# Reordering a feed-forward turn: route, choice and mixing ahead of the masked passes, the input sums at its start

## The chip, the core and the metric

One core of a Trainium2 chip runs the whole kernel. The metric is the device time of one execution in microseconds, lower is better. Engines are named as in the profile: PE (TensorE matmul), PEld (its weight loads), DVE (VectorE), ACT (ScalarE), POOL (GpSimd), SP (SyncE, which here only issues transfers).

## What is computed

An input x of shape (2, 4096, 256) goes through a feed-forward with half a residual, an attention, and the same feed-forward again:

```python
x = x + 0.5 * ffn(layernorm(x))
x = x + attention(layernorm(x))
x = x + 0.5 * ffn(layernorm(x))

def ffn(x):
    x_mixed = k[0] * x_before + k[1] * x + k[2] * x_behind        # along the sequence
    h = einsum('bsd,pdm->bspm', x_mixed, W1) + b1                  # 9 paths of width 64
    stacked = einsum('bspm,pmd->bspd', h, W2) + b2
    scores = tanh(x_mixed @ Wo1 + bo1) @ Wo2 + bo2
    collapsed = stacked of the path argmax(scores)
    return layernorm(x + collapsed) * gamma + beta
```

The change is in the feed-forward alone.

## The kernel before

Both feed-forwards (`ph` 0 and 1) run the same code over 16 tiles of 512 rows. Each engine's program is a list of turns, `for t in turns()`, from -6 to 16, fully unrolled, and inside a turn the order of the work is written out by hand, one `turn(t)` for each engine (DVE L814, ACT L1132, PE L1414, POOL L556, SP's loop behind L425). Engines meet only through semaphores. A turn works on several tiles at once, at the distances `STATS, ROWS, MIX, ROUTE, HIDDEN = 6, 5, 3, 2, 1`:

- tile t+6: DVE takes the input sums (`input_sums`, four BATCH_NORM_STATS2, recorded at L693) and moments (L700) of the rows in x; POOL makes scale and shift of them (`norm_scale`, L521 to L533).
- tile t+5: ACT writes the normalised rows n (L1071), PE transposes them (L1332), ACT copies the transposes to nT (L1077).
- tile t+3: ACT scales the middle tap of the mixing (L1085), DVE adds the tap before (`mixed_before`, L732) and behind (`mixed_behind`, L740), ACT rounds to f16 (`x_high`, L1093), DVE takes the remainder (`mixed_low`, L747).
- tile t+2: PE multiplies the hidden block 0 (`hidden(t, 0)`), which holds the scores' hidden layer and path 0; ACT does tanh (L1101) and keeps path 0 in hb (L1105); PE makes the nine scores (`route`, L1389); DVE finds the best in five small route steps (`route(t, 0)` to `route(t, 4)`, L777, L780, L784, L787, L790), which end in a one-hot; PE transposes it (`choice`, L1398), ACT copies it (`one_hot`, L1113), SP stores it to DRAM and loads it back three times as the mask of the tile (`spread`, L407 to L416).
- tile t+1: PE multiplies hidden blocks 1 to 4; DVE masks blocks 0 to 4 (`masked`, L802 and L805), ACT rounds them to f16 in three groups, blocks 0 and 1, 2 and 3, and 4 (`masked_high`, L1121), DVE takes the remainders (`masked_low` 0, 1 and 2, L811).
- tile t: PE multiplies by W2 (`path` 0 to 4). All split products on PE are at L1324.
- tile t-1: DVE adds the result to n (`result`, L753), ACT squares it (L1129), POOL makes 1/std (`result_scale`, L540 and L544), DVE scales it (`result_scaled`, four of L762) and adds x plus beta (`result_added`, L770), SP stores it (L423).

POOL's `residual` (L553) adds beta to the rows in x, 128x1024 f32, before `result_added` reads them. It waits for masked 3 of its tile.

x has eight tile buffers (`x_rows(t)` is t % NT, NT = 8). So SP loads tile t+7 in turn t, at the end of it, behind `store(t - 1)`, which waits for `result_added(t - 1)`, the last reader of that buffer. The input sums of tile t+7 come in turn t+1, in DVE's order behind masked 3. Tiles 0 to 7 of a feed-forward are loaded ahead of the turns (in the second, tiles 0 to 4 already within the attention).

PE has three banks for hidden blocks; `h_order` lists the blocks in PE's order, and each waits until the one three places earlier has been read. `hidden(t + ROUTE, 0)` opens PE's turn, `path(t, 4)` closes it. `path(t, 0)` waits for `result(t - 1)`, since both use the same two banks.

DVE's turn before, in order: result; masked 0, 1; mixed before (two); route 0; masked low 0; route 1; masked 2; route 2; mixed behind; route 3; mixed behind; route 4; masked 3; the four input sums; mixed low; masked 4; moments; masked low 1; result scaled (four); masked low 2; result added.

## Time and profile before

| what | us |
|---|---|
| median of three runs | 1528.1 (1524.33 to 1539.24) |
| profiled execution, its time | 1531.81 |
| profiled execution, span from first to last instruction | 1530.0 |
| first result pass to the last one, first feed-forward | 69.2 to 328.0 |
| the same, second feed-forward | 1271.1 to 1519.3 |

Shares of the span: PE 89%, DVE 79%, ACT 61%, POOL 20%; mean granted clock of PE 0.967. In the profile, starts are counted from the first instruction; an instruction's time overlaps the start of the next on its engine by some 0.1 us, so the time from start to start is what an instruction costs its engine. "idle before" is time in which an engine had nothing to run, and the name behind it is what ended that wait. PEclk is PE's granted clock, 1.00 being 2.4 GHz and 0.50 being 1.2 GHz.

### The profile page before, as it was taken

The numbers are of one execution on the slowest core, as the hardware profiler recorded it, in microseconds if no ns is written. First come the engines' busy times: TensorE is split into PE (matmuls) and PEld (weight loads), VectorE is DVE, ScalarE is ACT, GpSimd is POOL, SyncE is SP. The second block draws the span as 40 slices with busy tenths as digits, with TensorE's granted clock in tenths as the row PEclk, the third lists the DMA queues.
The fourth block names the chain that finished last, engine by engine and source line by source line (L and its number), as shares of the span: only waits on it lengthen the run. The fifth ranks groups of instructions, "written<-read, shape, count | busy, mean of one in ns | idle before, by whom it ended". The sixth has DMA issues, their size and how long they took to land.

```text
span 1530.0 us, 25980 instructions
## 1 busy us (share of the span) xinstructions
PE 1359.1 (89%) x7700; PEld 781.4 (51%) x7700; DVE 1215.7 (79%) x2349; ACT 936.8 (61%) x1745; POOL 306.9 (20%) x359
## 2 busy tenths in 40 slices
PE   4889988858999999999968999999998779989985
PEld 2556666544554454545344455454444346656653
DVE  6989999766677677677866767777678769999985
ACT  5656665326567666566855666766666666666642
POOL 2244452332001000000041101000000214444311
PEclk9989999979999999999989999999999879999997
DMA  5143333320000100102110011000103112333221
GB/s 155 43 118 88 90 101 113 90 69 1 28 29 15 41 14 15 32 11 74 37 43 1 28 42 42 0 28 0 42 0 110 56 32 61 103 97 106 61 74 57
DMA packets 86994, 82.26 MB, mean 54 GB/s; under 512 B 8540, under 2 KB 86885, under 8 KB 86885
## 3 DMA queue, kind: packets, MB, share of 16 engines
q1 hardware_dynamic: 86884, 80.91, 17.8%
q8 instruction: 56, 0.92, 0.3%
q14 instruction: 54, 0.43, 0.1%
HBM read 55.43 MB, written 25.46 MB: 53 GB/s over the span
## 4 chain that ended last, share of the span: by engine, by line
PE 62%; DVE 11%; DMA 10%; issue 7%; ACT 6%; SPq 2%; POOL 1%; DVEq 0%; ACTq 0%; POOLq 0%
PE PS L1324 55%; DMA R<-oh_scratch 7%; PE PS L1501 3%; DMA oh_scratch<-oh_t 2%; DVE R L753 2%; PE PS L1389 2%; PE PS L1332 1%; DVE R L770 1%; DVE R L937 1%; SPq L414 1%; SPq L412 1%; ACT oh_t L1113 1%; ACT R L1211 1%; ACT R L1215 1%; ACT R L1174 1%
## 5 line engine op out<-in xcount | busy, mean ns | idle before, releaser
L1324 PE MATMUL PS<-R 128*128 128x512 f16 (+3 forms) x3456 | 713.6, 361 | 27.4 <-DVE R L937 17.3
L1324 PEld LDWEIGHTS PS<-R 128*128 128x128 f16 (+1 forms) x3456 | 326.0, 98 | 392.3 <-DVE R L937 32.0
L1324 PE MATMUL PS<-w_hi,R 128*128 128x256 f16 x1280 | 239.1, 280 | 63.3 <-DVE R L753 63.1
L937 DVE TENSOR_TENSOR R<-R 128x512 f16<-128x512 f32 (+3 forms) x288 | 188.6, 655 | 111.5 <-ACT R L1215 110.3
L1202 ACT ACTIVATE R<-PS 128x512 f32 (+5 forms) x288 | 160.2, 558 | 162.7 <-PE PS L1324 162.2
L1324 PE MATMUL PS<-R,w_hi 128*128 128x512 f16 x640 | 198.0, 392 | 1.6 <-DVE R L747 1.5
L1211 ACT ACTIVATE R<-R 128x512 f32 (+4 forms) x288 | 169.5, 589 | 48.3 <-DVE R L931 46.8
L931 DVE TENSOR_TENSOR R<-R,max_row 128x512 f32 (+4 forms) x288 | 187.1, 650 | 7.7 <-ACT max_row L1248 7.7
L1215 ACT ACTIVATE R<-R 128x512 f16<-128x512 f32 (+3 forms) x288 | 171.1, 594 | 28.6 <-ACT R L1211 2.6
L925 DVE TENSOR_TENSOR run_max<-run_max,R 128x512 f32<-128x512 f32 (+3 forms) x272 | 173.9, 639 | 10.0 <-DVE run_max L925 1.7
L1324 PEld LDWEIGHTS PS<-w_hi,R 128*128 128x128 f16 x1280 | 128.4, 100 | 104.5 <-DVE R L753 77.1
L1324 PE MATMUL PS<-w_lo,R 128*128 128x256 f16 x640 | 179.0, 280 | 0.0
L1121 ACT ACTIVATE R<-R 128x1024 f16<-128x1024 f32 (+1 forms) x96 | 87.3, 909 | 146.4 <-DVE R L805 146.4
L521 POOL TENSOR_SCALAR veps<-mv 128x4 f32<-128x4 f32 x48 | 29.3, 610 | 690.5 <-DVE mv L700 631.0
L1324 PE MATMUL PS<-R,w_lo 128*128 128x512 f16 x320 | 124.7, 390 | 0.0
L805 DVE SCALAR_TENSOR_TENSOR R<-PS,b1c,R 128x512 f32<-128x512 f32 x128 | 95.0, 742 | 18.9 <-PE PS L1324 17.2
L811 DVE TENSOR_TENSOR R<-R 128x1024 f16<-128x1024 f32 (+1 forms) x96 | 98.4, 1028 | 2.4 <-ACT R L1121 2.4
L1332 PE MATMUL PS<-ident,R 128*128 128x128 f32 x384 | 64.3, 319 | 37.3 <-ACT R L1071 28.9
L553 POOL TENSOR_TENSOR R<-R,beta_b 128x1024 f32<-128x1024 f32 x32 | 75.7, 2365 | 105.5 <-DVE R L805 105.5
L1324 PEld LDWEIGHTS PS<-R,w_hi 128*128 128x128 f16 x640 | 63.8, 104 | 54.8 <-issue 7.1
L747 DVE TENSOR_TENSOR R<-R 128x1024 f16<-128x1024 f32 x32 | 73.9, 2310 | 2.9 <-ACT R L1093 2.9
L1332 PEld LDWEIGHTS PS<-ident,R 128*128 128x128 f32 x384 | 52.1, 164 | 47.0 <-issue 21.6
(109 smaller groups left out, 1555.3 us busy)
## 6 DMA issues: line engine op xcount, KB each, us to landing
R<-x_scratch SPq DMA_DIRECT2D x48, 512.0 KB, 4.5
x_scratch<-R SPq DMA_DIRECT2D x32, 512.0 KB, 3.2
R<-oh_scratch SPq DMA_DIRECT2D x32, 320.0 KB
R<-in_L_attn_x SPq DMA_DIRECT2D x16, 512.0 KB, 5.4
R<-oh_scratch SPq DMA_DIRECT2D x32, 256.0 KB
out<-R SPq DMA_DIRECT2D x16, 512.0 KB, 3.2
R<-in_L_ffn_W SPq DMA_DIRECT2D x2, 288.0 KB
R<-in_L_ffn_W SPq DMA_DIRECT2D x1, 512.0 KB
```

The lines of the kernel that those rows point to most:

```text
L553: g.tensor_tensor(rows4(x_rows(t)), rows4(x_rows(t)), beta_b[:, :].unsqueeze(1).to_broadcast([P, SUB, D]), ALU.add).then_inc(xb_done, 1)
L805: v.scalar_tensor_tensor(out=at, in0=ps_h[:, h_bank[g, c], :], scalar=b1c[:, c:c + 1], in1=chunk(mask, t, c), op0=ALU.add, op1=ALU.mult).t ...
L811: v.tensor_tensor(chunk(hlo, t, c, n), cols(hm, c * TT, n * TT), chunk(hhi, t, c, n), ALU.subtract)\
L925: v.tensor_tensor(run_max[:, lo:], run_max[:, lo:], cols(ring, at, TT - lo), ALU.max)\
L931: v.tensor_tensor(cols(ring, at, TT - lo), cols(ring, at, TT - lo), max_row[:, lo:], ALU.subtract)\
L937: v.tensor_tensor(p_lo[:, i * TT + lo:(i + 1) * TT], pf[:, (i % 2) * TT + lo:(i % 2 + 1) * TT], p_hi[:, i * TT + lo:(i + 1) * TT], ALU.sub ...
L1121: a.activation(chunk(hhi, t, c, n), cols(hm, c * TT, n * TT), ACT.Copy).then_inc(hhi_done, 1)
L1202: a.activation(cols(ring, ring_m + i * TT + lo, TT - lo), ps_s[:, i, lo:], ACT.Abs, scale=1.0 / (QS * XS * D ** 0.5)).then_inc(abs_done, 1)
L1211: a.activation(p, cols(ring, ring_n + i * TT + lo, TT - lo), ACT.Exp)\
L1215: a.activation(p_hi[:, i * TT + lo:(i + 1) * TT], p, ACT.Copy).then_inc(phi_done, 1)
L1324: ins = t_.matmul(dst, w, xx, start=start and n == 0, stop=stop and n == last, skip_group_check=skip)
L1332: ins = t_.transpose(dst[:, u * P:(u + 1) * P], cols(rows, u * D + c * P, P), ident[:, :])
```

## The change

DVE's turn after: result; route 0, input sum 0, route 1, input sum 1, route 2, input sum 2, route 3, input sum 3, route 4; mixed before (two); moments; mixed behind (two); masked 0, 1; mixed low; masked low 0; masked 2, 3, 4; masked low 1; result scaled; masked low 2; result added. PE opens with the scores (`route`) and puts the transposes of the one-hot (`choice`) behind path 0; hidden block 0 moves from the start of turn t+1 to the end of turn t, ahead of path 4. ACT takes tanh, the middle tap, squares, the one-hot, the normalised rows, x_high, then the three masked groups and nT. POOL's residual of tile t now waits for path 4 of tile t-1 (`o_psum`), and stands first in POOL's turn t. The mask loads count on two semaphores, one for even and one for odd tiles. Lines left out are marked by "...":

```diff
--- before.py
+++ after.py
@@ -35,6 +35,8 @@
...
 STATS, ROWS, MIX, ROUTE, HIDDEN = 6, 5, 3, 2, 1
+
+FIRST = ROUTE + 1
 
...
@@ -196,7 +198,7 @@
...
         route_psum, route_step, oh_done = sem("route_psum"), sem("route_step"), sem("oh_done")
-        ohT_psum, ohT_done, oh_stored, mask_in = sem("ohT_psum"), sem("ohT_done"), sem("oh_stored"), sem("mask_in")
+        ohT_psum, ohT_done, oh_stored, mask_in = sem("ohT_psum"), sem("ohT_done"), sem("oh_stored"), [sem("mask_in0"), sem("mask_in1")]
         hm_done, hhi_done, hlo_done = sem("hm_done"), sem("hhi_done"), sem("hlo_done")
...
@@ -345,8 +347,8 @@
...
             for t in turns():
-                h_order += [(use(ph, t + ROUTE), 0)] if on(t + ROUTE) else []
                 h_order += [(use(ph, t + HIDDEN), c) for c in range(1, HC)] if on(t + HIDDEN) else []
+                h_order += [(use(ph, t + FIRST), 0)] if on(t + FIRST) else []
         h_bank = {x: i % H_BANKS for i, x in enumerate(h_order)}
...
@@ -403,17 +405,17 @@
...
                     if g >= 2:
-                        sp.wait_ge(mask_in, 16 * MASK_LOADS * (g - 1))
+                        sp.wait_ge(mask_in[g % 2], 16 * MASK_LOADS * (g // 2))
                     sp.dma_start(there, oh_t[:, :]).then_inc(oh_stored, 16)
...
                     sp.dma_start(m[DM:P, :, :], there[0::2, :].unsqueeze(0).to_broadcast([DM, HC, TT]))\
-                        .then_inc(mask_in, 16)
+                        .then_inc(mask_in[g % 2], 16)
                     sp.dma_start(m[0:DM, 1:, :], there[1::2, :].unsqueeze(0).to_broadcast([DM, HC - 1, TT]))\
-                        .then_inc(mask_in, 16)
-                    sp.dma_start(m[0:NP, 0, :], there).then_inc(mask_in, 16)
+                        .then_inc(mask_in[g % 2], 16)
+                    sp.dma_start(m[0:NP, 0, :], there).then_inc(mask_in[g % 2], 16)
 
...
@@ -549,15 +551,14 @@
...
                     pool.wait_ge(n_done, k + 1)
-                    pool.wait_ge(hm_done, HC * k + 4)
+                    if t >= 1:
+                        pool.wait_ge(o_psum, k)
                     g.tensor_tensor(rows4(x_rows(t)), rows4(x_rows(t)),
...
                 def turn(t):
-                    if on(t - 1):
-                        result_scale(t - 1)
-                    if on(t + HIDDEN):
-                        residual(t + HIDDEN)
+                    if on(t):
+                        residual(t)
                     if on(t + STATS) and not early(ph, t + STATS):
...
@@ -566,6 +567,8 @@
...
                         first_scales(0, first_of(ph, t))
+                    if on(t - 1):
+                        result_scale(t - 1)
 
...
@@ -716,12 +719,15 @@
...
 
-                def input_sums(t):
+                def input_sum(t, u):
                     n = counted(ph, t)
-                    dve.wait_ge(x_in[t % NT], 16 * loads(ph, t))
-                    if n >= 2:
-                        dve.wait_ge(n_shift, n - 1)
-                    row_sums(X, t % NT * SUB * D, rows_set(ph, t), n_stat)
+                    if u == 0:
+                        dve.wait_ge(x_in[t % NT], 16 * loads(ph, t))
+                        if n >= 2:
+                            dve.wait_ge(n_shift, n - 1)
+                    ins = v.bn_stats(st[:, rows_set(ph, t), u, :], cols(x_rows(t), u * D, D))
+                    if u == SUB - 1:
+                        ins.then_inc(n_stat, 1)
 
...
@@ -797,7 +803,7 @@
...
                     if c == 0:
-                        dve.wait_ge(mask_in, 16 * MASK_LOADS * (g + 1))
+                        dve.wait_ge(mask_in[g % 2], 16 * MASK_LOADS * (g // 2 + 1))
                         dve.wait_ge(hb_done, g + 1)
...
@@ -818,43 +824,31 @@
...
                         result(t - 1)
+                    for i in range(SUB + 1):
+                        if choice:
+                            route(t + ROUTE, i)
+                        if rows and i < SUB:
+                            input_sum(t + STATS, i)
+                    if mix:
+                        mixed_before(t + MIX, 0)
+                        mixed_before(t + MIX, 1)
+                    if rows:
+                        input_moments(t + STATS)
+                    elif first_of(ph, t):
+                        first_stats(0, first_of(ph, t))
+                    if mix:
+                        mixed_behind(t + MIX, 0)
+                        mixed_behind(t + MIX, 1)
                     if here:
...
                     if mix:
-                        mixed_before(t + MIX, 0)
-                        mixed_before(t + MIX, 1)
-                    if choice:
-                        route(t + ROUTE, 0)
+                        mixed_low(t + MIX)
                     if here:
                         masked_low(t + HIDDEN, 0)
-                    if choice:
-                        route(t + ROUTE, 1)
-                    if here:
                         masked(t + HIDDEN, 2)
-                    if choice:
-                        route(t + ROUTE, 2)
-                    if mix:
-                        mixed_behind(t + MIX, 0)
-                    if choice:
-                        route(t + ROUTE, 3)
-                    if mix:
-                        mixed_behind(t + MIX, 1)
-                    if choice:
-                        route(t + ROUTE, 4)
-                    if here:
                         masked(t + HIDDEN, 3)
-                    if rows:
-                        input_sums(t + STATS)
-                    elif first_of(ph, t):
-                        first_stats(0, first_of(ph, t))
-                    if mix:
-                        mixed_low(t + MIX)
-                    if here:
                         masked(t + HIDDEN, 4)
-                    if rows:
-                        input_moments(t + STATS)
-                    if here:
                         masked_low(t + HIDDEN, 1)
...
@@ -1135,26 +1129,24 @@
...
                         act.wait_ge(w1_ready, 1)
+                    if choice:
+                        scores(t + ROUTE)
                     if mix:
                         middle(t + MIX)
-                    if choice:
-                        scores(t + ROUTE)
-                    if here:
-                        masked_high(t + HIDDEN, 0)
                     if last:
                         squares(t - 1)
+                    if choice:
+                        one_hot(t + ROUTE)
                     if on(t + ROWS):
...
                         x_high(t + MIX)
-                    if choice:
-                        one_hot(t + ROUTE)
                     if here:
+                        masked_high(t + HIDDEN, 0)
                         masked_high(t + HIDDEN, 1)
+                        masked_high(t + HIDDEN, 2)
                     if on(t + ROWS):
                         transposed(t + ROWS)
-                    if here:
-                        masked_high(t + HIDDEN, 2)
 
...
@@ -1412,19 +1404,17 @@
...
                 def turn(t):
-                    here, second, first = on(t), on(t + HIDDEN), on(t + ROUTE)
-                    if ph == 0 and t == -ROUTE:
-                        pe.wait_ge(w1_ready, 1)
+                    here, second, choose = on(t), on(t + HIDDEN), on(t + ROUTE)
                     if ph == 0 and t == 0:
                         pe.wait_ge(w2_ready, 1)
-                    if first:
-                        hidden(t + ROUTE, 0)
+                    if choose:
+                        route(t + ROUTE)
                     if second:
...
                         path(t, 0)
-                    if first:
-                        route(t + ROUTE)
+                    if choose:
+                        choice(t + ROUTE)
                     if second:
...
@@ -1433,14 +1423,17 @@
...
                         path(t, 2)
-                    if first:
-                        choice(t + ROUTE)
-                    if on(t + ROWS):
-                        transposed(t + ROWS)
                     if second:
...
                         path(t, 3)
+                    if on(t + ROWS):
+                        transposed(t + ROWS)
+                    if ph == 0 and t == -FIRST:
+                        pe.wait_ge(w1_ready, 1)
+                    if on(t + FIRST):
+                        hidden(t + FIRST, 0)
+                    if here:
                         path(t, 4)
```

## Rows read from the trace of the kernel before

**Rows 1.** Timeline of DVE in turn 6 of the first feed-forward (start us, us, engine, line, what).
```profile
161.08 1.21 DVE L753 SCALAR_TENSOR_TENSOR R<-PS,R 128x1024 f32<-128x1024 f32 x1
...
164.80 0.18 DVE L777 TENSOR_REDUCE r_max<-PS 128x4 f32<-128x36 f32 x1
164.91 1.21 DVE L811 TENSOR_TENSOR R<-R 128x1024 f16<-128x1024 f32 x1
...
168.58 0.75 DVE L805 SCALAR_TENSOR_TENSOR R<-PS,b1c,R 128x512 f32<-128x512 f32 x1
169.25 1.39 DVE L693 BATCH_NORM_STATS2 st<-R 128x6 f32<-128x256 f32 x4
170.56 2.37 DVE L747 TENSOR_TENSOR R<-R 128x1024 f16<-128x1024 f32 x1
...
174.91 1.66 DVE L762 SCALAR_TENSOR_TENSOR R<-R,y_rstd,gamma_b 128x256 f32<-128x256 f32 x4
...
178.24 1.21 DVE L753 SCALAR_TENSOR_TENSOR R<-PS,R 128x1024 f32<-128x1024 f32 x1
```

**Rows 2.** Timeline of PE in the same turn: path 0, route, hidden block 2, next path 0.
```profile
162.35 0.28 PE L1324 MATMUL PS<-w_hi,R 128*128 128x256 f16 x1 [1.80 <-DVE R L753]
...
163.67 0.96 PE L1389 MATMUL PS<-wo,th 65*128 65x9 f32 x8
164.48 0.59 PE L1324 MATMUL PS<-R,w_hi 128*128 128x512 f16 x2
...
179.50 0.28 PE L1324 MATMUL PS<-w_hi,R 128*128 128x256 f16 x1 [1.80 <-DVE R L753]
```

**Rows 3.** Instructions of L747 over the whole kernel (duration in ns min/median/max).
```profile
L747 DVE TENSOR_TENSOR R<-R x32: 1203/2370/3415, 23.9 to 1468.5; 128x1024 f16<-128x1024 f32 x32
```

**Rows 4.** Timeline of POOL in turn 6.
```profile
169.48 2.37 POOL L553 TENSOR_TENSOR R<-R,beta_b 128x1024 f32<-128x1024 f32 x1 [1.78 <-DVE R L805]
...
176.25 2.15 POOL L530 TENSOR_SCALAR neg<-mv 128x4 f32<-128x4 f32 x1
```

**Rows 5.** Timeline of ACT in turn 6.
```profile
170.70 1.04 ACT L1121 ACTIVATE R<-R 128x1024 f16<-128x1024 f32 x1
```

**Rows 6.** Timeline of SP at the start of turn 6.
```profile
161.19 0.41 SPq L423 DMA_DIRECT2D x_scratch<-R  x1
161.64 0.51 SPq L398 DMA_DIRECT2D R<-in_L_attn_x  x1
```

**Rows 7.** Transfer issues, 150 to 200 us and 1290 to 1440 us; then L398 alone, whole kernel.
```profile
R<-in_L_attn_x SPq DMA_DIRECT2D x3, 512.0 KB, 4.6
...
R<-x_scratch SPq DMA_DIRECT2D x8, 512.0 KB, 4.6
...
DMA to landing us min/median/max: 4.0/5.0/9.1
```

**Rows 8.** PE after two idle times, and windows beside them (busy us of PE, PEld, DVE, ACT, POOL; PEclk; DMA).
```profile
89.18 0.39 PE L1324 MATMUL PS<-w_hi,R 128*128 128x256 f16 x1 [2.86 <-DVE R L753]
...
1510.07 0.40 PE L1324 MATMUL PS<-w_hi,R 128*128 128x256 f16 x1 [3.88 <-DVE R L753]
...
93.00:98.00 5.00, 5.00 (x19) 2.72 (x20) 3.33 (x8) 2.10 (x6) 1.23 (x2) 0.50 0.13 44
98.00:103.00 5.00, 5.00 (x36) 3.37 (x35) 3.52 (x8) 2.47 (x3) 2.14 (x1) 0.94 0.00 1
1510.00:1520.00 10.00, 9.17 (x60) 7.05 (x60) 3.63 (x7) 1.70 (x8) 1.21 (x2) 0.74 0.31 102
```

**Rows 9.** Timeline of DVE: result passes that open turns 2 and 10 of each feed-forward.
```profile
87.91 1.21 DVE L753 SCALAR_TENSOR_TENSOR R<-PS,R 128x1024 f32<-128x1024 f32 x1
...
229.70 1.21 DVE L753 SCALAR_TENSOR_TENSOR R<-PS,R 128x1024 f32<-128x1024 f32 x1
...
1288.99 1.21 DVE L753 SCALAR_TENSOR_TENSOR R<-PS,R 128x1024 f32<-128x1024 f32 x1
...
1426.29 1.21 DVE L753 SCALAR_TENSOR_TENSOR R<-PS,R 128x1024 f32<-128x1024 f32 x1
```

## The prediction

> **What bounds the kernel now.** I read the page first for the engines' shares, then the Vector engine's timeline for one feed-forward turn, then SyncE's, GpSimd's and TensorE's timelines for the same turn. Vector is without a gap: the turn whose result pass starts at 161.08 ends when the next one starts at 178.24, 17.16 us, and nearly all of turns 2 to 9 of each feed-forward, which matter below, repeat it (this is turn 6 of the first) [rows 1]. TensorE idles 1.80 us in it, waiting for the result pass (L753), and works 15.35 us [rows 2]. So Vector sets the pace, and one of its instructions is slower than its kind: L747 takes 2.37 us as a rule and 1.20 at best [rows 3]. GpSimd's residual pass (L553, 169.48 to 171.85) lies across its start at 170.56 [rows 1, 4]; L747 ends 1.08 us after that pass does. Vector thus loses 1.17 us a turn to GpSimd. The input sums (L693) just ahead of it, beside the same pass, take 1.39 us for four and lose nothing.
>
> **The change part by part.** All offsets are from the start of the result pass.
>
> GpSimd's pass. It now waits for the end of the previous tile's paths (o_psum) instead of masked 3, and comes beside the result pass (1.14 us to the next start) and the input sums. L747 goes back to 1.20: minus 1.17. What could come late instead is route step 2, with two small operands in SBUF, at offset 2.0: at most the rest of the pass, 0.4 us, and nothing where the input sums wait longer than the pass lasts (below). The Trainium skill (GPSIMD Engine Reference, Key points) says that GpSimd contends with Vector instructions that have two SBUF inputs; the rows agree for L747. By that rule alone, the result pass, with one input in PSUM, would be free of it, as I take it; no row shows that pair, and its price is bounded by 0 and by the pass itself, 2.37.
>
> Masked passes in one run. Masked low 1 now stands right behind masked 4. It needs ScalarE's copy of the group of masked 3, 1.04 us [rows 5], and only masked 4 (0.67 us from start to start [rows 1]) lies between: about 0.5 us of new wait, counting 0.1 for two handovers. Masked low 0 has mixed low in front (1.1 us) against the same copy: 0.1. The bounds are 0, if the copies finish early, and 1.2, if nothing covers them.
>
> Input sums first. This is the part that decides. SyncE issues the store of x1 and then the load of tile t+7 only when the last pass of turn t (L770) is over, since that pass reads the buffer which the load overwrites: 161.19 and 161.64, that is 0.1 and 0.55 us behind the start of the next turn's result pass [rows 6]. The load lands 4.6 us after its issue, in the first feed-forward and in the second [rows 7], so at offset 5.15. Today the first input sum of that very tile stands at 169.25, offset 8.2, and the load has 3 us to spare. After the change it stands behind the result pass and route step 0, at 1.14 + 0.11 = 1.25 (a route step takes 0.11 from start to start, 164.80 to 164.91 [rows 1]). Vector waits from 1.25 to about 5.2: 3.95 us. Nothing hides it: Vector executes in order, and route steps 1 to 4, the mixing and all masked passes are queued behind that sum. The wait falls on tiles 8 to 15, the ones reloaded into the eight x buffers, so on turns 2 to 9 of either feed-forward: 16 turns. Turns 0 and 1, and those past 9, need no such load. The store issued just before the load shares the transfer engines with it; the bounds are the quickest and the slowest landing of that line, 4.0 and 9.1 us [rows 7]; I take the 4.6 of these very stages.
>
> The Trainium skill (DMA: Bandwidth & Descriptors, Rules for kernel authors) says to issue a transfer early and to wait for it late; this edit does the opposite for the x load. The same page (Anatomy of one DMA, Where 436 GB/s comes from) gives 2 us of fixed cost and some 358 GB/s from HBM; my estimate from that is 3.5 us for 512 KB, which would make the wait 2.85 and the total 18 us less. The trace's 4.6 us is used.
>
> Vector's turn by itself: 17.16 - 1.17 + 0.6 + 3.95 = 20.5 us, and about 0.1 more for handovers. I take 20.6.
>
> Route and choice first. The choice's transposes on TensorE now follow path 0. Path 0 starts at 1.27 and takes 1.32, route 0.81, a hidden block 1.3 [rows 2]. So TensorE is through path 0 at 2.6 and then has to wait for the one-hot (route step 4). The four sums (1.39 us) and steps 1 to 4 (0.45) follow the load, so that is done at about 7.1. TensorE stands still from 2.6 to 7.2, 4.6 us in one piece. It has 15.35 - 1.3 - 0.8 - 1.3 = 11.95 us of work left of the turn and is done at 19.2, 1.4 us before Vector. At the full clock this wait costs nothing.
>
> But the clock falls in such gaps. TensorE idled 2.86 us before 89.18, and the granted clock was 0.50 from 93 to 98 and 0.94 from 98 to 103, so at the lower of the two levels (1.2 GHz) until about 98.6, 9.4 us after it went on [rows 8]. Before 1510.07 it idled 3.88 us, and the clock was 0.74 in the stretch 1510 to 1520, which is 5.2 us at the lower level [rows 8]. Half the speed for 5.2 to 9.4 us costs TensorE 2.6 to 4.7 us; the 1.4 of slack takes a part, which leaves 1.2 to 3.3 a turn; 0 if the clock holds. I take 1.4, near the shorter one, because the gaps will come in every turn and recoveries can't all be long. The turn becomes 22.0 us.
>
> The per-parity mask semaphores add no instruction. The masks' way (store of the one-hot, three loads) starts some 1.5 us earlier in the turn and is used later: cost 0. The loads are no longer in flight just ahead of the x load. Beginning hidden 0 at the end of the turn instead of the start of the next is the same work; turn 2 of today's first feed-forward holds that loss of clock at 89.18, and its time is in the sum below as it was.
>
> Turns past 9. TensorE no longer transposes new tiles, so o_psum comes 1 to 2 us sooner and can meet Vector's four scaled-result instructions (L762), two SBUF inputs each. GpSimd's pass then takes its 2.2 us out of Vector in some turns: 0 to 4 turns in each feed-forward, 0 to 18 us, and against it L747's loss goes in those turns too. I take plus 8. The fill gains the waits for masks and loses at the mix: 0, give or take 3.
>
> **Sum.** Turns 2 to 9 last 229.70 - 87.91 = 141.8 us in the first feed-forward and 1426.29 - 1288.99 = 137.3 in the second [rows 9], 279.1 together. 16 x 22.0 = 352.0: plus 73. With the end's 8 and 3 less for turns 0 and 1: plus 78. The profiled execution took 1531.8 us (span 1530.0), the median of the runs is 1528.1: 1610 for a profiled one, 1606 as a median.
>
> **The rivals.**
> 1. The wait for the load alone, the clock holds. For: TensorE's slack of 1.4 us hides a short loss, and the gap of 1.80 before 179.50 [rows 2] goes by in every turn. Against: the gaps will be 4.6 us, and those of 2.86 and 3.88 each cost the clock. 16 x 20.6 = 330: plus 51, 1579 or, with the end's share gone, 1574.
> 2. GpSimd's pass gets hold of SBUF before the result pass. o_psum comes about 1.4 us before Vector's turn ends, while it is in L770 or one pass ahead of it. For: nothing in the code ties the pass to the result pass. Against: a small GpSimd instruction that began at 176.25, beside L762, ended only at 178.40 (2.15 us), when the next result pass had begun at 178.24 [rows 1, 4]: the two-input passes between had kept it out, and the same two (masked low 2, L770) stand there after the change. Should the pass go first, Vector loses 2.2 us in nearly every turn, part of which covers the clock's loss: 16 x 23 + 10 x 2, about plus 110: 1635.
> 3. The other side: the load is there in time and the kernel gets faster. The turn would then be 20.6 - 3.95 = 16.65, and 16 turns 266 instead of 279, minus 13, with the end about minus 8: 1520. It decides from a wait under 0.5 us, that is with the load landed at offset 1.8. Against: it is issued at 0.55 and the quickest took 4.0 us. For: only that the wait of one line is not yet in any trace.
>
> **How the numbers follow.** The forecast (load plus clock) 0.58, rival 1 0.22, rival 2 0.13, rival 3 0.04, and 0.03 for no change by some mixture. A measurement tells about 1% from no change here. Slower by over 1%: 0.93; within 1%: 0.04; faster: 0.03. The range: down to 1565 (clock holds, the load at 4.0 us), up to 1645 (rival 2, or 9 us of low clock each turn).
>
> **What would show it.** Right: the first L693 of turns 2 to 9 waits some 4 us for the x load (DMA R<-in_L_attn_x or x_scratch), turns of 21 to 23 us; TensorE's L1398 waits over 4 us for L790; L747 at 1.2 us; the granted clock under 0.9 in these turns. Wrong: no idle time ahead of L693, or turns below 18 us. A residual pass that begins while L762 runs, with L762 or L770 over 2 us long, would be rival 2; a clock of 1.00 beside 20.6 us turns rival 1.

## The result, and the profile after

| | median us (range) | profiled execution: time, span | PE clock |
|---|---|---|---|
| before | 1526.21 (1524.13 to 1539.24) | 1531.81, 1530.0 | 0.967 |
| after | 1606.98 (1603.35 to 1610.81) | 1607.41, 1605.6 | 0.947 |

The ratio is 1.0511, with a 95% interval of 1.0446 to 1.0575: 5% slower. The forecast said 1606.

I read the profile after in the order of the prediction: Vector's timeline, SyncE's, TensorE's, the clock by stretches, and then the ends, which the forecast had treated lightly. Lines have moved: L753, L693, L747, L762 and L398 of before are L759, L728, L753, L768 and L400 now.

Vector in turn 6 of the first feed-forward, which answers to [rows 1] (timeline of DVE; start us, us, engine, line, what, idle time before and its releaser):

```profile
176.78 1.22 DVE L759 SCALAR_TENSOR_TENSOR R<-PS,R 128x1024 f32<-128x1024 f32 x1
...
181.91 0.43 DVE L728 BATCH_NORM_STATS2 st<-R 128x6 f32<-128x256 f32 x1 [3.82 <-DMA R<-in_L_attn_x]
...
187.93 1.23 DVE L753 TENSOR_TENSOR R<-R 128x1024 f16<-128x1024 f32 x1
...
192.33 0.75 DVE L811 SCALAR_TENSOR_TENSOR R<-PS,b1c,R 128x512 f32<-128x512 f32 x1 [0.70 <-PE PS L1316]
```

The next result pass starts at 197.45, so this turn took 20.67 us instead of 17.16. The first input sum stands idle for 3.82 us; mixed low takes 1.23 us instead of 2.37. SyncE's timeline says why the sum waits:

```profile
176.89 0.41 SPq L425 DMA_DIRECT2D x_scratch<-R  x1
177.34 0.51 SPq L400 DMA_DIRECT2D R<-in_L_attn_x  x1
```

The group of the sums over the whole kernel (busy us, mean ns, then all idle time before them by releaser) says how much that is in all:

```profile
L728 DVE BATCH_NORM_STATS2 st<-R 128x6 f32<-128x256 f32 x108 | 44.2, 418 | 73.0 <-DMA R<-in_L_attn_x 34.7 <-DMA R<-x_scratch 33.4 <-issue 4.6
```

The load is issued 0.56 us behind the start of the result pass and the sum runs at 5.13, against 0.55 and 5.15 in the prediction. 34.7 + 33.4 = 68.1 us are 17 waits; 1.9 us of it belongs to the kernel's very first load, and the 16 waits of turns 2 to 9 are 66.2 us, 4.1 us each (3.6 to 5.5).

TensorE, which answers to [rows 2] (timeline of PE):

```profile
183.77 0.59 PE L1390 MATMUL PS<-ident,oh 128*9 128x128 f16 x4 [4.02 <-DVE oh L796]
```

The granted clock around it and over turns 2 to 9 (windows: stretch, its us, busy us and count of PE, PEld, DVE, ACT, POOL, then PEclk, DMA share, GB/s):

```profile
179.00:183.70 4.70, 0.75 (x7) 0.42 (x5) 1.79 (x9) 0.74 (x4) 0.10 (x1) 0.97 0.50 141
183.70:187.00 3.30, 3.23 (x12) 1.35 (x13) 3.30 (x10) 2.60 (x6) 1.40 (x2) 0.52 0.01 3
187.00:190.00 3.00, 3.00 (x24) 2.12 (x22) 2.97 (x4) 1.96 (x2) 2.82 (x3) 1.00 0.63 171
...
111.33:134.70 23.37, 17.89 (x113) 11.64 (x112) 16.14 (x33) 11.67 (x23) 8.39 (x8) 0.85 0.24 72
176.78:197.45 20.67, 16.65 (x113) 11.01 (x112) 16.12 (x33) 11.67 (x23) 8.40 (x8) 0.92 0.29 81
...
89.90:261.30 171.40, 135.99 (x876) 89.61 (x873) 129.00 (x257) 92.41 (x175) 67.19 (x57) 0.89 0.27 78
1328.54:1500.97 172.43, 136.35 (x876) 89.92 (x873) 128.96 (x257) 92.44 (x175) 67.17 (x57) 0.89 0.26 78
```

TensorE stands 4.02 us, then works at 0.52, the lower level (1.2 GHz), for some 3.3 us; masked 4 pays with 0.70 us of waiting. Over turns 2 to 9 the clock is 0.89 in both feed-forwards.

The turn read is one of the milder ones. The last two pairs of lines show turn 3, turn 6, and turns 2 to 9 of either feed-forward. Ten of the 16 turns have a clock of 0.92, which is 3.3 us at the lower level, and take 20.9 us on average; the other six have 0.84 or 0.85, which is some 7 us at the lower level, and take 22.5. Turn 3, with 0.85, takes 23.37 us: its load lands 6.0 us behind its issue, so that the first sum waits 5.27 us, and masked 4 waits 1.92 us for TensorE.

**Where the 75.6 us of span came from**, by the starts of the result passes (before against after): turns 2 to 9, 141.8 to 171.4 and 137.3 to 172.4, together +64.7, a mean turn of 21.5; from turn 10 to the last result pass +5.1 and +1.0; turn 1, 18.7 to 16.9 and 17.8 to 16.9, -2.8; and the stretches ahead of the first result pass of each feed-forward, +3.8 and +3.8 (69.22 to 73.02, and from the last result pass of the first feed-forward to the first of the second, 943.1 to 946.9). That is 64.7 + 6.1 - 2.8 + 7.6 = 75.6.

### The profile page after: what moved, and what is told of

It reads as the page before. It is cut to its first block, busy times and chain, and to the rows that moved or that the text cites. A ratio compares the mean times of both kernels' runs of the same rounds, so it can differ in the third digit from the quotient of the medians.

```text
span 1605.6 us, 25980 instructions
## 1 busy us (share of the span) xinstructions
PE 1385.4 (86%) x7700; PEld 789.3 (49%) x7700; DVE 1202.7 (75%) x2349; ACT 944.0 (59%) x1745; POOL 334.0 (21%) x359
## 4 chain that ended last, share of the span: by engine, by line
PE 60%; DVE 20%; issue 6%; ACT 6%; DMA 5%; SPq 1%; POOL 1%; ACTq 0%; DVEq 0%; POOLq 0%
PE PS L1316 54%; PE PS L1494 3%; DVE R L768 3%; DMA R<-x_scratch 2%; DMA R<-in_L_attn_x 2%; DVE R L817 2%; DVE R L776 2%; DVE R L811 2%; DVE st L728 2%; DVE R L931 1%; PE PS L1324 1%; ACT R L1203 1%; ACT R L1115 1%; ACT R L1207 1%; ACT R L1166 1%
## 5 line engine op out<-in xcount | busy, mean ns | idle before, releaser
L1316 PE MATMUL PS<-w_hi,R 128*128 128x256 f16 x1280 | 253.2, 287 | 36.4 <-DVE R L759 36.4
L1316 PE MATMUL PS<-R,w_hi 128*128 128x512 f16 x640 | 210.3, 413 | 5.6 <-DVE R L753 2.9
L523 POOL TENSOR_SCALAR veps<-mv 128x4 f32<-128x4 f32 x48 | 17.8, 370 | 828.3 <-DVE mv L703 671.2
L1316 PE MATMUL PS<-w_lo,R 128*128 128x256 f16 x640 | 183.6, 287 | 0.0
L1316 PEld LDWEIGHTS PS<-w_hi,R 128*128 128x128 f16 x1280 | 132.3, 103 | 79.6 <-DVE R L759 41.9
L1316 PE MATMUL PS<-R,w_lo 128*128 128x512 f16 x320 | 131.9, 412 | 0.0
L556 POOL TENSOR_TENSOR R<-R,beta_b 128x1024 f32<-128x1024 f32 x32 | 91.5, 2860 | 187.5 <-PE PS L1316 187.5
L728 DVE BATCH_NORM_STATS2 st<-R 128x6 f32<-128x256 f32 x108 | 44.2, 418 | 73.0 <-DMA R<-in_L_attn_x 34.7
L1123 ACT ACTIVATE R<-R 128x256 bf16<-128x256 f32 x128 | 51.6, 404 | 71.0 <-DVE R L759 71.0
```

Of the source, the lines that this page charges most:

```text
L556: g.tensor_tensor(rows4(x_rows(t)), rows4(x_rows(t)), beta_b[:, :].unsqueeze(1).to_broadcast([P, SUB, D]), ALU.add).then_inc(xb_done, 1)
L1316: ins = t_.matmul(dst, w, xx, start=start and n == 0, stop=stop and n == last, skip_group_check=skip)
```

## The experiments

Each run is given with its ratio to the kernel before, taken on the same chip, and with "T", the mean length of turns 2 to 9 of both feed-forwards by the starts of the result passes. For comparison: before T = 17.4 (with one turn of 21.7 us at a clock of 0.76; 17.16 otherwise), after T = 21.5.

**1. The sums behind the mixing.** The kernel after, with the four sums and the moments moved:

```diff
-                        if rows and i < SUB:
-                            input_sum(t + STATS, i)
                     if mix:
                         mixed_before(t + MIX, 0)
                         mixed_before(t + MIX, 1)
+                        mixed_behind(t + MIX, 0)
+                        mixed_behind(t + MIX, 1)
                     if rows:
+                        for u in range(SUB):
+                            input_sum(t + STATS, u)
                         input_moments(t + STATS)
...
-                    if mix:
-                        mixed_behind(t + MIX, 0)
-                        mixed_behind(t + MIX, 1)
```

> The changed kernel with one part undone: the four input sums and the moments stand behind the mixing again (offset about 5.5 us of a turn), the five route steps back to back in front. If the wait for the x load is the cause, it ends before the sums come: the idle time ahead of the input sums (3.85 us in the changed kernel) falls below 0.3 us, PE's gap ahead of the one-hot transposes to under 1.5 us, the clock stays up, turns 2 to 9 take 17.2 to 17.6 us (not less than before, since route step 2 now stands in GpSimd's pass), and the kernel comes to 1530 to 1550 us. If another part of the change carries the loss (the masked passes in one run, the later choice), turns stay over 20 us and the kernel over 1590 us.

Measured: 1574.65 us, ratio 1.0296 (1.0264 to 1.0327), T = 19.0. The load's wait is nearly gone (none in seven of the 16 turns, 0.2 to 1.0 us in eight, 1.7 in one) and the time falls by 32 us, but this is far above the 1530 to 1550 expected. Turns of about 17.6 and 19.96 us mostly alternate. Vector's and GpSimd's timelines in a long turn and at the start of a short one:

```profile
164.18 3.77 DVE L768 SCALAR_TENSOR_TENSOR R<-R,y_rstd,gamma_b 128x256 f32<-128x256 f32 x4
...
183.88 1.67 DVE L768 SCALAR_TENSOR_TENSOR R<-R,y_rstd,gamma_b 128x256 f32<-128x256 f32 x4
...
164.66 2.62 POOL L556 TENSOR_TENSOR R<-R,beta_b 128x1024 f32<-128x1024 f32 x1 [2.61 <-PE PS L1315]
...
185.55 3.95 POOL L556 TENSOR_TENSOR R<-R,beta_b 128x1024 f32<-128x1024 f32 x1 [3.80 <-PE PS L1315]
```

Where GpSimd's pass falls among the four scaled-result passes, these take 3.77 us instead of 1.67. That is the prediction's rival 2, which the load's wait had hidden in turns 2 to 9: with Vector 3.9 us late, o_psum never came so early in Vector's turn. Where the pass is ready one step later (185.55), behind the scaled results, it records 3.95 us and keeps waiting while masked low 2 and the result's addition run one behind the other.

**2. The load ahead of the store.** The kernel after, with SyncE's two issues swapped:

```diff
-                        store(t - 1)
...
+                            sp.wait_ge(x1_done, use(ph, t - 1) + 1)
                             load_rows(t - 1 + NT)
+                        store(t - 1)
```

> The changed kernel with the x load issued ahead of the store on SyncE, both still behind the last reader of the buffer. Load theory: issued 0.45 us sooner and with the store behind it instead of in front, it lands 3.2 to 3.7 us after the start of the result pass instead of 5.1, the wait of the input sums falls to 2.0 to 2.5 us, each of the 16 turns by 1.4 to 1.9 us or a little more with the clock, and the kernel to 1570 to 1585 us. If the wait were set by something else (the shared input path, n_shift), nothing changes: 1603 to 1611 us.

Measured: 1593.58 us, ratio 1.0419 (1.0387 to 1.0451), T = 20.5. SyncE's issue, the waits of the sum and of masked 4 (DVE), and the one-hot's (PE), in the timelines of one turn:

```profile
173.62 0.40 SPq L400 DMA_DIRECT2D R<-in_L_attn_x  x1
...
178.00 0.43 DVE L731 BATCH_NORM_STATS2 st<-R 128x6 f32<-128x256 f32 x1 [3.17 <-DMA R<-in_L_attn_x]
...
189.65 0.75 DVE L814 SCALAR_TENSOR_TENSOR R<-PS,b1c,R 128x512 f32<-128x512 f32 x1 [1.93 <-PE PS L1319]
...
179.86 0.59 PE L1393 MATMUL PS<-ident,oh 128*9 128x128 f16 x4 [3.59 <-DVE oh L799]
```

The load's landing in turns 2 to 9 of the first feed-forward, in the kernel after and then in this run:

```profile
DMA to landing us min/median/max: 4.5/4.6/6.0
...
DMA to landing us min/median/max: 4.2/4.4/4.5
```

The load is issued 0.45 us sooner and lands 0.2 us faster (the medians of the second feed-forward are 4.5 and 4.3). It is there 4.49 us behind the start of the result pass, not at the 3.2 to 3.7 expected, and that is why the 13 us won are less than the 22 to 37 expected. The wait shrinks by 0.65 us in the turn read and by 0.9 on average (4.1 to 3.2), and T falls by 1.0. The turns swing between 19.6 and 21.4: those at a clock of 1.00 take 19.6 to 19.9 us, those at 0.84 take 21.2 to 21.4, with masked 4 waiting 1.93 us for TensorE in the one read.

**3. TensorE kept busy in the gap.** The kernel after, with hidden block 2 multiplied three more times ahead of the choice in turns 2 to 9 (same bank, same values, about 3.9 us of extra work at the full clock):

```diff
                         path(t, 0)
+                    if 2 <= t <= 9:
+                        for i in range(3):
+                            hidden(t + HIDDEN, 2, spare=True)
                     if choose:
```

> The changed kernel, where PE repeats hidden block 2 three times more (3.9 us, into the bank that the real one then overwrites) in turns 2 to 9, between path 0 and the choice, where it waits. Adds work to PE and takes none away. Clock theory: the gap shrinks from 4.0 us to about 0.4, the granted clock stays at 1.00 in turns 2 to 9, the turns fall from 21.5 us on average to 20.5, the kernel by 12 to 20 us to 1587 to 1595 us. If the clock's fall costs nothing (PE's slack covers it), the time stays within 4 us of the changed kernel, 1603 to 1611 us, or rises.

Measured: 1593.21 us, ratio 1.042 (1.0389 to 1.0451), T = 20.5, as the clock theory wanted. The window of a turn, and of turns 2 to 9:

```profile
173.96:194.41 20.45, 19.25 (x130) 12.28 (x128) 16.09 (x33) 11.47 (x22) 9.59 (x8) 1.00 0.28 82
...
91.62:255.90 164.28, 154.10 (x1026) 98.26 (x1024) 128.82 (x257) 91.81 (x176) 76.76 (x57) 1.00 0.29 82
1323.84:1487.16 163.32, 154.10 (x1026) 98.25 (x1024) 128.82 (x257) 91.81 (x176) 76.77 (x57) 1.00 0.28 82
```

TensorE has more to do and the kernel is 14 us faster. Every turn now takes 20.3 to 20.8 us: Vector's own turn with the load's wait in it, which the prediction had put at 20.6. The fallen clock costs 21.5 - 20.5 = 1.0 us a turn. About 0.3 of that is the load's wait, 3.9 us on average here and 4.1 in the kernel after: the late landings of the long turns are gone too. Why a load lands late there was not tried.

**4. GpSimd's pass tied to the result pass.** The kernel after, with one wait more on the residual pass, for the last pass of Vector's previous turn:

```diff
                         pool.wait_ge(o_psum, k)
+                        pool.wait_ge(x1_done, k - 1)
```

> The changed kernel, where GpSimd's residual pass also waits for x1_done of tile t-2, the last DVE pass of the turn before, so that it can't start beside the scaled result. Theory that the pass is let in between those instructions and holds them (four turns over 3.7 us for L768 in the changed kernel, 2.1 us each): all L768 groups take 1.67 us, and the turns past 9 get faster by 8 to 12 us in sum; turns 2 to 9 unchanged within 0.1 us each. Kernel 1595 to 1601 us. If those groups are long for another reason: unchanged, 1603 to 1611 us.

Measured: 1596.14 us, ratio 1.0447 (1.0414 to 1.048), T = 21.3 (21.32 against 21.49): as expected. All 32 passes of GpSimd now take 2.34 to 2.37 us (2.34 to 4.41 in the kernel after), and at the ends the scaled results take 1.67 us again instead of 3.77. From turn 10 to the last result pass the two feed-forwards are 5.0 and 5.2 us shorter than in the kernel after.

**5. Both: the sums behind the mixing and the pass with the result.**

> The kernel after with both of the earlier edits: the input sums and moments behind the mixing, and GpSimd's residual pass made to wait for the last pass of Vector's previous turn as well. The theory says that the first edit alone took away the wait for the load and let GpSimd's pass in among the four scaled-result passes in every second turn, which costs those turns 2.1 to 2.4 us (turns of 17.6 and 19.96 us in turn). With the second edit the pass starts beside the result pass in every turn, so all of turns 2 to 9 should take 17.2 to 18.0 us: 1.2 us less over 16 turns, 19 us, and some 10 us at the ends, as the second edit gave alone: 1540 to 1550 us from 1574.65. The rival (the long turns come from something else, as a late hidden block or the clock) has them stay at 17.6 and 20.0 in turn: 1565 to 1575.

Measured: 1548.67 us, ratio 1.014 (1.0103 to 1.0176), T = 18.3, with 13 of the 16 turns at 18.15 to 18.17. The alternation is gone, and so the 2.1 us in every second turn were GpSimd's. But 18.16 us a turn is above the 17.2 to 18.0 expected. The start of a turn in the timelines of DVE and POOL:

```profile
166.39 1.21 DVE L760 SCALAR_TENSOR_TENSOR R<-PS,R 128x1024 f32<-128x1024 f32 x1
167.52 0.18 DVE L784 TENSOR_REDUCE r_max<-PS 128x4 f32<-128x36 f32 x1
167.74 0.20 DVE L787 TENSOR_TENSOR r_eq<-PS,r_max 128x36 f32<-128x36 f32 x1
167.97 1.09 DVE L791 TENSOR_TENSOR r_pr<-r_eq,prio 128x36 f32<-128x36 f32 x1
169.09 0.19 DVE L794 TENSOR_REDUCE r_top<-r_pr 128x4 f32<-128x36 f32 x1
169.31 0.20 DVE L797 TENSOR_TENSOR oh<-r_pr,r_top 128x36 f16<-128x36 f32 x1
...
166.64 2.36 POOL L557 TENSOR_TENSOR R<-R,beta_b 128x1024 f32<-128x1024 f32 x1 [5.71 <-DVE R L777]
```

Route step 2 (L791), with its two operands in SBUF, is held for 0.89 us by the rest of GpSimd's pass; result pass and steps 0 and 1, which have one operand in PSUM, run through it. And a step that needs the one just before it starts 0.22 us behind it (not counting the held time), where a step followed by other work takes 0.11 [rows 1]: the four handovers cost some 0.4. With masked low 1's wait for its copy, 0.46, and about 0.25 of small gaps, 17.16 - 1.17 + 0.89 + 0.4 + 0.46 + 0.25 = 18.0; the turn is 18.16. So the route in one block costs 1.3 us a turn in itself. In the kernel after neither the held step nor the handovers show, since the sums lie between the steps and the load's wait outlasts the pass.

**6. Before, with nothing but the sums moved** right behind the result pass:

```diff
                         result(t - 1)
+                    if rows:
+                        input_sums(t + STATS)
```

> The kernel before with one edit: the four input sums stand right behind the result pass. Theory: the wait for the x load is a loss by itself, whatever the order of the rest: the first sum at offset 1.15, the load there at about 5.2, so 4 us a turn in turns 2 to 9, the masked passes and the mixing late by that. Turns of 21 to 22.5 us, L747 at 1.2 or 2.4 by where GpSimd's pass falls: 1528.6 plus 16 times 3.8 to 5.3: 1590 to 1613 us. The rival, that the wait costs only together with the choice in front (TensorE's gap), has Vector catch up: 1528 to 1560 us.

Measured: 1626.6 us, ratio 1.0648 (1.061 to 1.0687), T = 23.2: slower than the whole change, and above the expected range. DVE, then PE and POOL:

```profile
167.05 1.41 DVE L693 BATCH_NORM_STATS2 st<-R 128x6 f32<-128x256 f32 x4 [3.98 <-DMA R<-in_L_attn_x]
...
175.81 3.24 DVE L747 TENSOR_TENSOR R<-R 128x1024 f16<-128x1024 f32 x1 [0.36 <-ACT R L1093]
180.00 0.75 DVE L805 SCALAR_TENSOR_TENSOR R<-PS,b1c,R 128x512 f32<-128x512 f32 x1 [0.96 <-PE PS L1324]
...
174.85 0.59 PE L1398 MATMUL PS<-ident,oh 128*9 128x128 f16 x4 [4.21 <-DVE oh L790]
...
175.60 2.36 POOL L553 TENSOR_TENSOR R<-R,beta_b 128x1024 f32<-128x1024 f32 x1 [1.44 <-DVE R L805]
```

One edit brings the whole loss: 3.98 for the load; mixed low 0.87 longer and 0.36 idle, since with the sums no longer ahead of it GpSimd's pass lies across all of it; and TensorE's gap of 4.21 with masked 4's wait of 0.96 behind it. 17.16 + 3.98 + 0.87 + 0.36 + 0.96 = 23.3. The rival, that the wait needs the choice in front to hurt, falls.

**7. Before, with nothing but GpSimd's pass moved** (it waits for o_psum and comes first in its turn):

```diff
-                    pool.wait_ge(hm_done, HC * k + 4)
+                    if t >= 1:
+                        pool.wait_ge(o_psum, k)
```

> The kernel before with one edit: GpSimd's residual pass waits for the end of the previous tile's paths instead of masked pass 3, and comes first in its turn. It lies beside the result pass then, and behind that stands masked 0, with two operands in SBUF. Theory: what L747 gets back (1.17 us a turn) masked 0 loses, by the rest of the pass, 1.0 to 1.3 us, so the time stays: 1520 to 1536 us. If the result pass covered GpSimd's altogether, the gain of 1.17 us in some 28 turns would stand whole: 1495 to 1500. If the pass gets in among the scaled-result passes, as it does in the kernel after without the load's wait, turns take 1 us more: 1545 to 1560.

Measured: 1551.93 us, ratio 1.0168 (1.0131 to 1.0204), T = 17.4. DVE and POOL in a turn of the middle, and POOL and DVE at the end:

```profile
175.89 1.21 DVE L754 SCALAR_TENSOR_TENSOR R<-PS,R 128x1024 f32<-128x1024 f32 x1
177.03 2.26 DVE L803 TENSOR_TENSOR R<-R 128x512 f32<-128x512 f32 x1
...
186.80 1.20 DVE L748 TENSOR_TENSOR R<-R 128x1024 f16<-128x1024 f32 x1
...
176.39 2.35 POOL L554 TENSOR_TENSOR R<-R,beta_b 128x1024 f32<-128x1024 f32 x1
...
1483.93 3.76 DVE L763 SCALAR_TENSOR_TENSOR R<-R,y_rstd,gamma_b 128x256 f32<-128x256 f32 x4
...
1484.79 2.62 POOL L554 TENSOR_TENSOR R<-R,beta_b 128x1024 f32<-128x1024 f32 x1 [9.37 <-PE PS L1325]
```

The middle goes by the theory: mixed low is at 1.20, and masked 0 behind the result pass takes 2.26 instead of 0.67. The whole is that of the third alternative, because past turn 9 the pass gets in among the scaled results, in one turn of the first feed-forward and five of the second (18.0 to 21.2 us a turn in the second feed-forward, against 15.7 to 16.9 before).

**8. A candidate: masked 1 beside GpSimd's pass.** The kernel after with the pass tied to the result pass; Vector's order is result, route 0, masked 1, route 1 to 4, mixing, sums, masked 0, mixed low, and the rest with the moments behind masked 3; `result_scale` ahead of `norm_scale`.

> A candidate. The order behind the result pass: route step 0, masked 1 (one operand in PSUM), route steps 1 to 4, mixing, input sums, masked 0, mixed low, masked low 0, masked 2 and 3, moments, masked 4, masked low 1; the residual pass beside the result pass by the added wait, result_scale ahead of norm_scale on GpSimd. The load has until offset 7 or so, masked 1 stands beside the rest of GpSimd's pass, L747's like takes 1.2 us, the copy for masked low 1 has the moments and masked 4 ahead of it. Theory: Vector's turn is 17.16 less 1.17 plus up to 0.8 of waits, 16.2 to 16.9 us: 1505 to 1530 us. If the theory on where the time goes lacks a part, it stays above 1535.

Measured: 1526.91 us, ratio 0.9999 (0.9978 to 1.002), T = 17.1. The time is in the expected range, the turn above the 16.2 to 16.9 expected. Step 2 is now held for 0.37 us only, and the load is in time but for 0.6 us in two turns. The change's whole loss is gone, but not more. A steady turn is 17.0 us: 17.16 - 1.17 + 0.37 for the held step, some 0.4 for the handovers and 0.20 for masked low 1's wait. What turns 2 to 9 win by it, the stretches ahead of the first result passes lose (73.8 us against 69.2 in the first feed-forward, 947.1 against 943.1 in the second).

**9. The pass behind route step 4.** The kernel before, its order untouched, with one wait changed:

```diff
-                    pool.wait_ge(hm_done, HC * k + 4)
+                    if on(t + ROUTE - HIDDEN):
+                        pool.wait_ge(oh_done, use(ph, t + ROUTE - HIDDEN) + 1)
+                    else:
+                        pool.wait_ge(hm_done, HC * k + 4)
```

> A version that should beat both. The kernel before, its order untouched, with one wait changed: GpSimd's residual pass waits for route step 4 (the one-hot of the tile ahead) instead of masked 3. It then starts 0.85 us earlier and lies beside masked 3 and the input sums, none of which it held up in any trace, so that mixed low, which lost 1.17 us a turn, loses only some 0.3. Theory: turns 16.3 us instead of 17.16 in turns 2 to 9, and 0.9 us less in the others, 28 turns in all: 1500 to 1512 us. If the pass gets in before masked 3's neighbours with two SBUF operands (the mixing ahead of step 4), or mixed low waits for its own inputs, the time stays: 1520 to 1530.

Measured: 1518.65 us, ratio 0.9952 (0.9935 to 0.9969), T = 16.9: a gain, but not the 15 to 28 us expected. DVE and POOL:

```profile
164.11 1.39 DVE L696 BATCH_NORM_STATS2 st<-R 128x6 f32<-128x256 f32 x4
165.42 1.55 DVE L750 TENSOR_TENSOR R<-R 128x1024 f16<-128x1024 f32 x1
167.46 0.75 DVE L808 SCALAR_TENSOR_TENSOR R<-PS,b1c,R 128x512 f32<-128x512 f32 x1 [0.49 <-PE PS L1327]
...
163.52 2.37 POOL L556 TENSOR_TENSOR R<-R,beta_b 128x1024 f32<-128x1024 f32 x1 [0.96 <-DVE oh L793]
```

Mixed low is at 1.55, as worked out. What the expectation left out is the wait that this uncovers: masked 4 arrives sooner than TensorE's hidden block 4, 0.49 us of idle time. And past turn 9 no input sums stand ahead of mixed low, so there the pass still lies across it (2.58 us in turn 10), where the expectation had counted 0.9 us a turn.

**10. The same, and the moments ahead of mixed low.**

> The run before this one and also the moments (0.29 us, no operand pair in SBUF) ahead of mixed low, so that nothing of GpSimd's pass is left when mixed low starts. Theory: 0.3 us less in turns with input sums, some 17 turns: 1496 to 1508 us, 4 to 6 us under the run with the wait alone. The rival: the moments stand right behind the sums they read and wait for them, or masked low 1 waits for its copy by what the moments no longer cover, and nothing is won: within 2 us of that run.

Measured: 1517.37 us, ratio 0.9933 (0.9908 to 0.9958), T = 16.9 (16.65 in the second feed-forward alone). Mixed low is at 1.19 us, masked 4 waits 0.32. By the medians within 2 us of the run before it, though its steady turns are 0.26 us shorter: turns 1 and 2 of the first feed-forward took 18.7 and 20.0 us in its profile (17.9 and 16.9 in run 9) and gave that back. On the whole time alone the two can't be told apart.

**11. The choice behind path 1.** Run 4, with the transposes of the one-hot moved on TensorE:

```diff
-                    if choose:
-                        choice(t + ROUTE)
                     if second:
                         hidden(t + HIDDEN, 2)
                     if here:
                         path(t, 1)
+                    if choose:
+                        choice(t + ROUTE)
```

> The kernel after with the added wait of the residual pass (as in the run in which the pass was tied to the result pass, 1596.14 us) and the choice's transposes moved on TensorE from behind path 0 to behind path 1. Theory: the clock falls for TensorE's 4 us in one piece; with hidden block 2 and path 1 ahead of the choice TensorE idles less in one piece, the clock stays high, and the turn is Vector's own with the load's wait, 20.5 us in turns 2 to 9: 1580 to 1588 us. The rival, that turns of 21 to 23 come from elsewhere than the clock after that gap, has 1593 to 1600.

Measured: 1604.16 us, ratio 1.0496 (1.0455 to 1.0536), T = 20.6: the whole is outside both expectations. The turns are what the theory said: T was 21.3 in run 4, TensorE stands 1.64 us for the one-hot in the turn read, instead of 3.8 to 5.4 (timeline of PE), and the clock is 0.99 (window of turns 2 to 9 of the second feed-forward):

```profile
170.54 0.39 PE L1391 MATMUL PS<-ident,oh 128*9 128x128 f16 x4 [1.64 <-DVE oh L797]
```

```profile
1332.85:1497.79 164.94, 127.62 (x880) 84.02 (x880) 128.84 (x257) 90.87 (x176) 65.30 (x56) 0.99 0.28 81
```

These 16 turns are 11 us shorter. But the first result pass comes at 80.7 us instead of 73.5, turn 1 takes 19.7 us instead of 16.9 in both feed-forwards, and from turn 10 to the last result pass they take 2.6 and 4.2 us more. The timeline of DVE ahead of the first result pass shows the way of it:

```profile
74.19 1.23 DVE L754 TENSOR_TENSOR R<-R 128x1024 f16<-128x1024 f32 x1 [5.38 <-ACT R L1088]
```

ScalarE copies the one-hot before it makes x_high, and executes that list in order. There it stands 7.90 us for the choice, and so mixed low waits 5.38 us for x_high, against 0.38 in run 4. Where Vector doesn't set the turn, a later one-hot is a later turn. The expectation had priced the steady turns alone.

**12. Hidden block 4 first.** Run 10, with TensorE's hidden block 4 ahead of the row transposes:

```diff
-                    if on(t + ROWS):
-                        transposed(t + ROWS)
                     if second:
                         hidden(t + HIDDEN, 4)
+                    if on(t + ROWS):
+                        transposed(t + ROWS)
```

> The better of the two runs with the pass behind route step 4 (moments ahead of mixed low, 1517.37 us, turns of 16.65 us) and hidden block 4 ahead of the row transposes on TensorE. In that run Vector does all its work of the turn without loss but one wait: masked 4 stands 0.32 us idle for TensorE's hidden block 4, which has eight transposes (0.93 us) ahead of it. Theory: that wait goes, the turn takes 16.3 to 16.4 us, some 17 turns: 1509 to 1514 us. The rival: the rows' transposes come late for ScalarE's copy and masked low 1 or 2 waits for its own copy in ScalarE's queue: no change or slower, 1516 to 1522 us.

Measured: 1506.47 us (1502.04 to 1509.09), ratio 0.9849 (0.9814 to 0.9884), T = 16.3. Faster than both kernels by more than the interval and below the 1509 to 1514 expected. The timelines of DVE and POOL:

```profile
177.20 0.75 DVE L808 SCALAR_TENSOR_TENSOR R<-PS,b1c,R 128x512 f32<-128x512 f32 x1
177.87 1.39 DVE L696 BATCH_NORM_STATS2 st<-R 128x6 f32<-128x256 f32 x4
179.41 0.38 DVE L703 BATCH_NORM_AGGREGATE mv<-st 128x2 f32<-128x6 f32 x4
179.70 1.19 DVE L750 TENSOR_TENSOR R<-R 128x1024 f16<-128x1024 f32 x1
...
177.27 2.37 POOL L556 TENSOR_TENSOR R<-R,beta_b 128x1024 f32<-128x1024 f32 x1 [0.96 <-DVE oh L793]
```

And the window of turns 2 to 9 of the second feed-forward:

```profile
1271.03:1401.01 129.98, 122.37 (x882) 84.57 (x880) 128.13 (x257) 90.62 (x177) 52.17 (x56) 1.00 0.35 103
```

From 177.27 to 179.64 GpSimd's pass lies beside masked 3, the sums and the moments, none of which it holds, and Vector's turn has no wait left.

## Why the prediction was right

Its mechanism is the one that the runs show, a wait for the load and a clock that falls in the gap behind it. That the time fits to 1 us (1606 against 1606.98) is luck: two of its terms were off by 8 us each, in opposite directions. Point by point:

- **The wait for the load** (3.95 predicted): 3.82 in the turn read, 4.1 on average. Right, and shown to be the main cause by undoing it (run 5 against run 4: 47.5 us, T from 21.3 to 18.3) and by doing it alone (run 6).
- **Vector's turn, 20.6**: 20.5 where the clock stood (run 3). The sum was right. Of its "0.6 of masked passes in one run", masked low 0 waits for nothing in the turn read, and masked low 1 waits 0.46 us where TensorE isn't late (run 5); the rest are small gaps.
- **GpSimd's pass, minus 1.17 and route step 2 free**: mixed low took 1.23, and step 2 was free. Its "at most 0.4" without the wait has no run. In run 5 step 2 is held for 0.89, but there it stands at offset 1.58, since the sums no longer lie between the steps, where the prediction had 2.0, and the pass, tied to the end of Vector's turn, ends at 2.61 instead of 2.4. That the result pass, with one operand in PSUM, goes free was left open there and is now seen: 1.21 us beside the pass in runs 5 and 7.
- **The clock, 1.4 a turn, bounds 1.2 to 3.3**: 1.0. This is one term that failed in size, and 1.0 lies below its bounds. The prediction took the time at the lower level from two gaps of before, 5.2 and 9.4 us; it is 3.3 us in ten turns, some 7 in six, and 4.7 on average (a clock of 0.89 over 21.5 us). Half of 4.7 less the slack of 1.4 is 0.95, close to the 1.0 measured: the working was sound and its input too long. The gap was 4.0 us in the turn read, against 4.6. That makes T 21.5 instead of 22.0, and the 16 turns 64.7 us instead of 73. The mechanism is shown by run 3 (more work, no gap, clock 1.00, 14 us less) and by the turns of run 11 (a short gap, clock 0.99, T less 0.7).
- **The turns past 9, plus 8**: +6.1. The mechanism is there as described: in five turns of the profile after, the four scaled results take 3.75 or 3.77 us instead of 1.67. Run 4 takes it away: 11 us.
- **Turns 0 and 1, minus 3**: -2.8 for turn 1.
- **The fill, 0, give or take 3**: +3.8 in either feed-forward, +7.6. The step that failed is "gains the waits for masks and loses at the mix". Before, Vector waits at masked 0, which the code lets wait for the mask loads, 1.53 us ahead of the first result pass and 1.62 in turn 1 of the first feed-forward; these waits are gone. But 3.5 of the 3.8 us are there already when Vector begins the tile work of turn -1 (44.63 against 41.17 us); 0.97 of it comes from later scores and 1.30 from a wait for x_high. From there turn -1 wins 0.85 us and turn 0 loses 1.2, with waits for x_high (0.38), the masked copy (0.46) and path 4 (1.24). In run 11 a later choice makes the stretch 7.3 us longer than in run 4, by way of x_high. That speaks for the chain from tile to tile; which link of it costs the 3.8 us was not tried.

Of the rivals, the first (clock holds, 1574) is out by the clock of 0.89. Its time doesn't follow from its terms, which give 1579 without the ends and 1584 with them; run 3, in which the clock does hold, took 1593, since the two fills are 10 us longer as well. The second is real but does not decide, since the load's wait keeps it out of turns 2 to 9. The third, the load in time, has no run in the change's own order. Runs 1, 5 and 8 bring the load in time by moving the sums, and none of them came to its 1520. Its turn of 16.65 compares with 18.16 in run 5 and 17.0 in run 8, where the sums no longer part the route steps, so that the handovers and the held step come on top.

The prediction's estimate from the Trainium skill (DMA: Bandwidth & Descriptors, Anatomy of one DMA and Where 436 GB/s comes from) was 3.5 us for the load. The fixed cost in it is the Trainium skill's figure for a transfer that GpSimd issues, and this load is issued by SyncE. The trace has 4.6 and 4.5 us in the median of turns 2 to 9 behind a store of the same size, and 4.4 and 4.3 ahead of it (run 2), so the measurement stands. The Trainium skill (GPSIMD Engine Reference, Key points) names Vector instructions with two SBUF inputs among those that contend; every held instruction here was of that kind (mixed low, masked 0, route step 2, the scaled results), and the result pass, the PSUM steps and the sums beside a pass were not held.

## What to carry to other kernels

When work is moved forward in an in-order engine, look at where its input comes from: a load that is issued at the end of one turn landed 4.4 to 6.3 us later here, wherever its reader stood, and the reader's wait falls on everything queued behind it and on the next engine's clock. A wait of that length also hides other losses, so undoing it gives back less than its length (run 1). Of the four places tried for GpSimd's pass the best was the one tied by a wait to the Vector instruction ahead of a stretch of sums and of work with one operand in PSUM: one changed wait, and two neighbours put in order, together were worth 1.5%, where a reordering of the whole turn cost 5%.

## What the runs showed of the hardware that was not expected

- A pass of GpSimd that becomes ready while Vector runs instructions one behind the other gets in among the four scaled-result instructions (3.77 us instead of 1.67, five times in the profile after), but not between masked low 2 and the result's addition (its record grows to 3.95 us in run 1). What tells these two apart was not tried.
- A small Vector instruction that needs the result of the one just before it starts 0.22 us behind it; where other work lies between, the small instruction costs 0.11 from start to start (runs 5 and 9).
- Extra work on TensorE made the kernel faster by 14 us (run 3): the granted clock went from 0.89 to 1.00 in turns 2 to 9, and T from 21.5 to 20.5.
- With a store and a load of 512 KB each issued some 0.45 us apart on one queue, their order hardly mattered to the load and much to the store: in turns 2 to 9 of the first feed-forward the load's median landing is 4.6 us as the second and 4.4 as the first (run 2), the store's 3.2 as the first and 5.2 as the second.
